# Three places of a two-layer gated cross-attention kernel: the first value block, the end of the first attention, and the LoRA tail

## The reference

```python
x = x + tanh(g_xattn[0]) * L0_xattn(layernorm(x), ctx, ctx, ...)   # rope, mask, softmax, 32 heads on 8 key heads, D = 128
x = x + tanh(g_ffn[0])   * L0_ffn(layernorm(x), ...)               # 16 experts, top 2
x = x + tanh(g_xattn[1]) * L1_xattn(layernorm(x), ctx, ...)        # RMS-normed queries and keys
x = x + tanh(g_ffn[1])   * L1_ffn(layernorm(x), ...)               # 4 LoRA experts of rank 16, top 2

# L1_ffn
logits = flat @ Wr.T                      # top 2 of 4, softmax over them: gates
mid = einsum('tf,erf->ter', flat, A)
delta = sum_e gates[:, e] * (mid_e @ B_e.T) * 4
```

## Time and profile before

| what | value |
| --- | --- |
| median of 3 runs | 1242.37 us (1242.19 to 1243.41) |
| profiled execution, own time | 1242.58 us |
| its span, first to last instruction | 1240.4 us |
| busy: PE, weight loads, DVE, ACT, POOL | 96%, 77%, 67%, 34%, 47% |

### The profile page before, as it was taken

The page is one execution under the profiler, slowest core; times in us unless marked ns, Lnnn a source line. Parts: engine busy times, 40 slices in busy tenths (PEclk is TensorE's granted clock), DMA queues, the critical chain, the costliest instruction groups (busy, mean ns, idle before and its releaser), DMA issues.

```text
span 1240.4 us, 16897 instructions
## 1 busy us (share of the span) xinstructions
PE 1194.8 (96%) x6188; PEld 949.3 (77%) x6188; DVE 828.4 (67%) x1446; ACT 423.9 (34%) x734; POOL 577.7 (47%) x399
## 2 busy tenths in 40 slices
PE   7999999899999999999899999999999999999997
PEld 6887878677777778777678887777777777777776
DVE  4656644978788887788963225586566757656795
ACT  5144151322212222222344113534444443444432
POOL 4431431757667676675344112335454545545500
PEclk9999999999999999999999999999999999999999
DMA  7844625522121221212110002122122212211101
GB/s 271 254 149 149 211 101 180 205 86 77 49 78 68 85 76 43 78 40 76 69 60 35 1 0 86 60 79 76 51 76 76 76 44 74 76 51 37 74 1 68
DMA packets 57584, 106.86 MB, mean 86 GB/s; under 512 B 3776, under 2 KB 36544, under 8 KB 52160
## 3 DMA queue, kind: packets, MB, share of 16 engines
q1 hardware_dynamic: 57008, 105.17, 24.7%
q0 software_dynamic: 384, 1.05, 0.2%
q10 hardware_dynamic: 144, 0.00, 0.0%
HBM read 78.95 MB, written 27.26 MB: 86 GB/s over the span
## 4 chain that ended last, share of the span: by engine, by line
PE 70%; DVE 13%; POOL 8%; issue 6%; ACT 3%; DMA 0%; POOLq 0%; DVEq 0%; ACTq 0%
PE ps_b L226 11%; PE ps_b L227 11%; PE ps_b L228 11%; PE ps_q L226 9%; PE ps_q L227 9%; PE ps_q L228 9%; DVE r_s L1317 3%; PE ps_b L950 2%; PE ps_s L923 2%; POOL qT L1199 2%; POOL wo_lo L1192 2%; POOL wq_lo L717 1%; PE ps_q L910 1%; POOL p_sb L769 1%; DVE o_lo L1360 1%
## 5 line engine op out<-in xcount | busy, mean ns | idle before, releaser
L226 PE MATMUL ps_q<-hT_hi,wq_hi 128*128 128x512 f32 x512 | 207.2, 405 | 4.6 <-ACT qT L1066 4.1
L227 PE MATMUL ps_q<-hT_lo,wq_hi 128*128 128x512 f32 x512 | 200.1, 391 | 0.0
L228 PE MATMUL ps_q<-hT_hi,wq_lo 128*128 128x512 f32 x512 | 199.6, 390 | 0.0
L226 PE MATMUL ps_b<-wo_hi,o_hi 128*128 128x512 f32 x440 | 172.9, 393 | 6.4 <-POOL wo_lo L1192 6.4
L227 PE MATMUL ps_b<-wo_lo,o_hi 128*128 128x512 f32 x440 | 172.1, 391 | 0.0
L228 PE MATMUL ps_b<-wo_hi,o_lo 128*128 128x512 f32 x440 | 171.9, 391 | 0.0
L1199 POOL TENSOR_TENSOR qT<-q_t 128x512 f32<-128x512 f32 x64 | 88.8, 1387 | 91.3 <-DVE q_t L1295 91.3
L226 PEld LDWEIGHTS ps_q<-hT_hi,wq_hi 128*128 128x128 f32 x512 | 96.1, 188 | 40.8 <-issue 13.5
L1360 DVE TENSOR_TENSOR o_lo<-ps_b,o_hi 128x512 fp32r<-128x512 f32 x128 | 82.1, 684 | 65.4 <-ACT o_hi L1104 64.0
L1369 DVE SCALAR_TENSOR_TENSOR x_sb<-ps_b,gates,x_sb 128x512 f32<-128x512 f32 x120 | 86.1, 724 | 52.9 <-PE ps_b L228 52.3
L717 POOL TENSOR_TENSOR wq_lo<-wq_raw,wq_hi 128x512 fp32r<-128x512 f32 x64 | 89.3, 1399 | 56.3 <-ACT wq_hi L711 56.3
(11 more groups left out here) (271 smaller groups left out, 2488.6 us busy)
## 6 DMA issues: line engine op xcount, KB each, us to landing
wq_raw<-in_wq SPq DMA_DIRECT2D x16, 1024.0 KB, 4.8
wo_raw<-in_wo SPq DMA_DIRECT2D x16, 1024.0 KB, 4.9
kT<-kT_spill SPq DMA_DIRECT2D x32, 256.0 KB, 3.4
v_hi<-v_hi_spill SPq DMA_DIRECT2D x16, 512.0 KB, 3.7
v_lo<-v_lo_spill SPq DMA_DIRECT2D x16, 512.0 KB, 4.6
v_hi_spill<-vs_hi SPq DMA_DIRECT2D x12, 512.0 KB, 5.9
v_lo_spill<-vs_lo SPq DMA_DIRECT2D x12, 512.0 KB, 6.7
kw_raw<-in_wk SPq DMA_DIRECT2D x4, 1024.0 KB, 8.9
```

The source lines that it names most:

```text
L226: nc.tensor.matmul(dst, l_hi, r_hi, start=first, stop=False)
L227: nc.tensor.matmul(dst, l_hi, r_lo, start=False, stop=False)
L228: return nc.tensor.matmul(dst, l_lo, r_hi, start=False, stop=last)
```

## The change

**Start.** TensorE runs 20 transposes of the identity into a free bank (`WARM`). Then, within a slice, high x high of all four tiles comes first, once the high parts are there, then context high x weights low, then context low x weights high.

**End of the first attention.** GpSimd subtracts the maxima of unit 14 ahead of the query addition (15, 2). VectorE does rotations 2 and 3 of unit 15 and the sums of unit 14 ahead of the last two low halves of unit 13. After the last low half of unit 15 it does output addition 0, four norms and low halves 0 and 1, then the other additions.

**Tail.** The token product takes all 128 columns of `a_raw`. Routing is done for tiles 0 to 3, then 4 to 6, then 7. ScalarE multiplies `b_raw` by `gate_l` once, so VectorE only adds. Tile 7's x is put into a bank by a product with the identity, its delta is accumulated there, and ScalarE copies the sum to x. Product 7 waits until VectorE has read the logits of tiles 4 to 6.

```diff
 def kv_pe(pe):
+    pe.wait_ge(prep["ident"], 1)
+    for n in range(WARM):                                  # WARM = 20
+        nc.tensor.transpose(ps_b[2][:, 0:P], ident[:, :], ident[:, :])
     for k in range(KC):
-        pe.wait_ge(c["w0_lo"], k + 1)
-        pe.wait_ge(prep["ctx_lo"], k + 1)
-        for i in range(4):
-            last = three(kv_banks[i][:, :], cT_hi[...], cT_lo[...], kw_hi[0][:, k, :], kw_lo[0][:, k, :], k == 0, k == KC - 1)
+        parts = (("hi", "hi"), ("hi", "lo"), ("lo", "hi"))
+        for ctx_part, w_part in parts:
+            ...
+            for i in range(4):
+                last = nc.tensor.matmul(kv_banks[i][:, :], ...)
```

```diff
 # GpSimd, att_pool, step
                 added(1)
+                if before_closing(lay, g, h):
+                    att_shift(pool, lay, us)
                 added(2)
 # VectorE, att_dve, first attention
                 rotate(last, 1, 2)
+                rotate(last, 1, 3)
+                sums(last - 1)
             out_low(last - 2, 2)
             out_low(last - 2, 3)
-            if lay == 0:
-                rotate(last, 1, 3)
-            sums(last - 1)
+            if lay:
+                sums(last - 1)
...
+            add_output(last, 1, 0)
             ln_rs(dve, ln, 0)
             ln_norm(dve, ln, 0)
             ln_norm(dve, ln, 1)
-            for t in range(PAIRS):
-                add_output(last, 1, t)
-                ln_stat(dve, ln, PAIRS + t, added)
-                for i in LN_BESIDE[t]:
-                    ln_low(dve, ln, i)
-                    if i + 2 < PAIRS:
-                        ln_norm(dve, ln, i + 2)
+            ln_stat(dve, ln, PAIRS, added)
+            ln_norm(dve, ln, 2)
+            ln_norm(dve, ln, 3)
+            ln_low(dve, ln, 0)
+            ln_low(dve, ln, 1)
+            for t in (1, 2):
+                add_output(last, 1, t)
+                ln_stat(dve, ln, PAIRS + t, added)
+            ln_low(dve, ln, 2)
+            ln_low(dve, ln, 3)
+            add_output(last, 1, 3)
+            ln_stat(dve, ln, PAIRS + 3, added)
```

```diff
 # tail
-                last = nc.tensor.matmul(bank[:, (i % PAIRS) * P:(i % PAIRS) * P + LN], xT[...], a_raw[:, k, 0:LN], ...)
+                last = nc.tensor.matmul(bank[:, (i % PAIRS) * P:(i % PAIRS + 1) * P], xT[...], a_raw[:, k, :], ...)
...
+                nc.scalar.activation(b_raw[:, :], b_raw[:, :], ACT.Copy, scale=gate_l[:, 0:1]).then_inc(lora["b_s"], 1)
...
 # lora_pe
             gated_t(0)
+            pe.wait_ge(c["route"], route_steps[PAIRS] + 1)
             lora_mid(pe, NT - 1)
-            pe.wait_ge(c["b_in"], 32)
+            pe.wait_ge(c["b_s"], 1)
             deltas(0)
+            pe.wait_ge(lora["gated"], 1)
+            nc.tensor.matmul(mid_banks[0][:, :], ident[:, :], x_sb[:, NT - 1, :], start=True, stop=False)
             gated_t(1)
             deltas(1)
 # lora_act, at its end
+            act.wait_ge(c["delta"], NT)
+            nc.scalar.activation(x_sb[:, NT - 1, :], delta_bank(NT - 1)[:, :], ACT.Copy).then_inc(c["x_last"], 1)
 # lora_dve
-            route(1)
-            dve.wait_ge(c["gate_l"], 1)
-            add_output(0)
+            route(PAIRS, NT - 1)
+            route(NT - 1, NT)
             gate(1)
-            for i in range(1, NT):
+            for i in range(NT - 1):
                 add_output(i)
```

More of the change, by code:

```diff
@@ L503, in kv_pe @@
             c = kv
+            pe.wait_ge(prep["ident"], 1)
+            for n in range(WARM):
+                nc.tensor.transpose(ps_b[2][:, 0:P], ident[:, :], ident[:, :])
             for k in range(KC):
-                pe.wait_ge(c["w0_lo"], k + 1)
-                pe.wait_ge(prep["ctx_lo"], k + 1)
-                for i in range(4):
[L509 to L512, removed]
+                parts = (("hi", "hi"), ("hi", "lo"), ("lo", "hi"))
+                for ctx_part, w_part in parts:
+                    if (ctx_part, w_part) == ("hi", "hi"):
+                        pe.wait_ge(c["w_hi"], k + 1)
+                        pe.wait_ge(prep["ctx_hi"], k + 1)
+                    elif w_part == "lo":
+                        pe.wait_ge(c["w0_lo"], k + 1)
+                    else:
+                        pe.wait_ge(prep["ctx_lo"], k + 1)
+                    for i in range(4):
+                        last = nc.tensor.matmul(kv_banks[i][:, :], (cT_hi if ctx_part == "hi" else cT_lo)[:, k, i * P:(i + 1) * P],
+                                                (kw_hi if w_part == "hi" else kw_lo)[0][:, k, :], start=k == 0 and (ctx_part, w_part) == parts[0],
+                                                stop=k == KC - 1 and (ctx_part, w_part) == parts[2])
+                        if k == KC - 1 and (ctx_part, w_part) == parts[2]:
+                            last.then_inc(c["tile"], 1)
             pe.wait_ge(prep["ctx_lo"], 2 * KC)
@@ L1942, in lora_sync @@
             for i in range(NT):
[L1943 removed]
+                sp.wait_ge(*((c["x_added"], i + 1) if i < NT - 1 else (c["x_last"], 1)))
                 sp.dma_start(ot[:, i, :], x_sb[:, i, :]).then_inc(c["out"], 16)
@@ L1991, in lora_mid @@
             for k in range(KC):
-                last = nc.tensor.matmul(bank[:, (i % PAIRS) * P:(i % PAIRS) * P + LN], xT[:, k, i * P:(i + 1) * P], a_raw[:, k, 0:LN],
+                last = nc.tensor.matmul(bank[:, (i % PAIRS) * P:(i % PAIRS + 1) * P], xT[:, k, i * P:(i + 1) * P], a_raw[:, k, :],
                                         start=k == 0, stop=k == KC - 1)
@@ L2087, in lora_act, with route @@
             gated_copy(1)
+            act.wait_ge(c["delta"], NT)
+            nc.scalar.activation(x_sb[:, NT - 1, :], delta_bank(NT - 1)[:, :], ACT.Copy).then_inc(c["x_last"], 1)
         def lora_dve(dve):
             c = lora
[L2091 to L2098 removed]
+            def route(i0, i1):
+                own, tiles, n = slice(i0, i1), range(i0, i1), i1 - i0
+                mid = mid_banks[i0 // PAIRS].rearrange("p (i m) -> p i m", m=P)[:, i0 % PAIRS:i0 % PAIRS + n, :]
+                done = route_steps[i0]
                 dve.wait_ge(c["l_clear"], 2)
[L2100 to L2101 removed]
+                dve.wait_ge(*lns[3]("rs", RS_PARTS.index((i0, i1)) + 1))
+                dve.wait_ge(c["mid"], i1)
                 nc.vector.tensor_tensor(l_lg[:, own, 0:LX], mid[:, :, LM:LN], wide(ln_rs_sb[:, own], LX), ALU.mult).then_inc(c["route"], 1)
@@ L2123, in gate @@
                 mid = mid_banks[h].rearrange("p (i m) -> p i m", m=P)
-                done = steps * h + 4 + 2 * PAIRS
+                done = gate_steps[h]
                 dve.wait_ge(c["l_ex"], h + 1)
```

45 lines of the change are left out of this document (21 added, 24 removed).

## The result

| kernel | median of its runs | lowest and highest | ratio to before, 95% interval |
| --- | --- | --- | --- |
| before | 1242.51 us (6 runs) | 1242.01, 1243.41 | |
| after | 1235.59 us (6 runs) | 1234.18, 1237.65 | 0.9945 [0.9934, 0.9956] |

What follows compares the result with a forecast made beforehand. TensorE was taken to bound the kernel, seven tenths of the last-ending chain. From the profiled 1242.58 us, start -2.3, attention's end -4.1 and tail -0.4 gave 1235.8 us, range 1234.2 to 1239.6.

Steps and rivals of the forecast that it cites:

- Start, -2.3: Program start: earlier first matmul and earlier upper clock, less a new wait, start tile 4 at 18.4 instead of 20.66 us.
- wait at tile 4: Start: the first four tiles finish close together, so tile 4 waits 0.9 us for tile 0's eviction from bank 0.
- The two slow matmuls that I allowed for: Start: the clock rises at 6.87 us, so only two real matmuls run slowly, costing 0.4 us.
- B: Rival at the start: transposes do not bring the clock forward, start gains only 0.2 us, total 1237.9 us, chance 0.28.
- Softmax, -1.95: First attention's end: GpSimd's earlier shift for unit 14 lets its transpose start at 595.35 instead of 597.30 us.
- Norms, -2.15: Norms for the MoE: VectorE's reordering brings the router product 2.15 us forward, -4.1 together with the softmax part.
- The wait ahead of the router product: MoE's start: the old wait becomes one of 1.2 us, for low half 3, ahead of the router product.
- the lower clock hardly matters: Norms stretch, clock 0.50 at 636: the new 1.2 us wait can hide it, so whether it goes hardly matters.
- Tail, -0.4: Tail: additions end at 1236.9 instead of 1237.97 us, but queued stores leave an end 0.4 us earlier.
- The upper clock in the last deltas: Tail: last deltas take about 1.0 us at the upper clock, giving -0.4; 2.08 at the lower, giving +0.4.
- only the last two stores queue for their data: Tail: two stores issued 0.45 us apart queue for their data, which reduces the gain to 0.4 us.
- a shift passes whole to the end: Between the edited stretches: TensorE has no gap or waits only on its own earlier work, so shifts reach the end whole.

Runs made afterwards that it cites:

- no_warm: The changed kernel without the twenty transposes at the start, order of the passes kept; median 1237.97 us, ratio 0.9962.
- fill: The changed kernel with transposes of the identity put into four stalls of TensorE (at 178, 245, the MoE's end, the tail); median 1232.35 us, ratio 0.9924.
- fill_before: The kernel before with transposes filling its stalls at 180, 248, the MoE's end and ahead of values 14 (601); median 1239.11 us, ratio 0.9973.
- after_again: The changed kernel run once more, nothing altered; median 1235.91 us, ratio 0.9944.
- tail_only: The kernel before with the new tail alone; median 1242.31 us, ratio 1.0 [0.999, 1.001].
- cols68: The changed kernel with 68 instead of 128 columns in the tail's token products; median 1234.40 us, ratio 0.9936.
- start_attn: The changed kernel with the old tail, so new start and attention's end only; median 1235.71 us, ratio 0.9945.
- start_only: The kernel before with the new start alone (twenty transposes, reordered passes); median 1241.56 us, ratio 0.9993 [0.9983, 1.0003].
- act01: The changed kernel with output tiles 0 and 1 also written by ScalarE through identity products, like tile 7; median 1236.55 us, ratio 0.9955.

## Why the prediction was right, point by point

**Start, -2.3: right, with a spread that I left out.** First real matmul 6.14 (6.18), wait at tile 4 0.83 (0.9), tile 4 at 18.15 (18.4). The two slow matmuls that I allowed for were none in one profile, about three in the other. B's 20.5 for tile 4 without transposes was 19.90, since eight matmuls were slow, not twelve. The rule of the Trainium skill, "TensorE: Matmul & The Clock Gate", section "Part 4: PE-mode transpose", that the upper clock doesn't engage for transposes, isn't what these runs show: without the transposes (no_warm) eight matmuls were slow that weren't in after, and in fill 26 transposes kept the granted clock at 1.00 behind 245, where after had 0.50.

**Softmax, -1.95: right.** The shift starts at 582.69, ahead of rotation 2; values 14 gained 1.9 more, and the wait is 0.75 (0.7).

**Norms, -2.15: right in the mechanism, off in size.** It measured 2.7 and 2.6 us (fill). The wait ahead of the router product is 0.98 (1.2): VectorE's chain was half a microsecond shorter than my sum. But I didn't ask what the low clock of before cost there. By fill_before, where it didn't fall, 1.46 of the 2.6 are the clock that fell behind the wait of 1.73, and 1.2 the reordering itself. So over half of the term was that the edit took a stall away. My sentence that the lower clock hardly matters spoke of the kernel after, where the new wait would hide it; no profile of a kernel with this edit has the low clock there, so it stays untested.

**Tail, -0.4: about right, by wrong steps.** Filled, the new tail is 0.2 us faster than the old (1232.35 and 1232.54), which their runs hardly tell apart. The upper clock in the last deltas was a chance: up in after, down in after_again. And I let only the last two stores queue for their data, while all eight leave within 5 us and take 2.3 us to land instead of 2.0 in fill, tail_only and cols68. The new tail took 26.5 to 26.6 us from its first token products in tail_only, cols68, no_warm and fill, the old one 26.9 to 27.7 in the six kernels that have it. In five of these the clock fell before the last delta had ended, and the sixth has the long end told below, so no two profiles compare the tails at equal clocks. Between before and fill it is 0.3 us.

The 28.3 us of after are not the tail's order. Between fill's profile and after's, the stores' end differs by 1.7 us. Here are windows of 1 us in after behind its last delta, the share of its DMA queues from 1224.3 to 1233.3 us, and a window of fill behind its last delta:

```profile
1228.00:1229.00 1.00, 0.00 (x0) 0.00 (x0) 0.09 (x1) 0.00 (x0) 0.00 (x0) 1.00 0.56 211
1231.00:1232.00 1.00, 0.00 (x0) 0.00 (x0) 0.00 (x0) 0.00 (x0) 0.00 (x0) 0.81 0.28 105
1232.00:1233.00 1.00, 0.00 (x0) 0.00 (x0) 0.00 (x0) 0.00 (x0) 0.00 (x0) 0.50 0.03 12
...
q8 instruction: 1, 0.02, 0.9%
```

```profile
1228.00:1229.00 1.00, 0.00 (x0) 0.00 (x0) 0.00 (x0) 0.00 (x0) 0.00 (x0) 1.00 1.02 387
```

In after the traffic halves once amid the stores and trickles at their end, and a packet of 16 KB of the instruction queue lies among them. Three of the fourteen profiles have such a packet while stores are under way: after, after_again and start_attn. In these three 3.9 to 5.2 us pass from the last write of x to the end of the span. In the other profiles with the new tail it is 3.3 to 3.5 us, in the other ones with the old tail 2.5. So the long end goes with that packet, in the old tail as in the new, and the new one's own price at the stores is 0.8 to 1.0 us, which its earlier last write makes up for. No run moves the packet, so that it is the cause is not shown.

**What the sum didn't have.** The MoE's end (-1.64 in after) is no term of it. In the profile the start brought -2.5, the softmax part -1.8, the norms -2.7, the MoE's end with small shifts behind it -1.5, and the tail +1.4: in all -7.1. I had said that a shift passes whole to the end, since TensorE runs without a gap between the stretches. That step failed: start_only kept 1.0 of its 2.4 us up to 590, and each of the eight unfilled profiles with those edits won 1.6 to 1.7 at the MoE's end, which I hadn't counted. The total came out right by luck: 1.5 at the MoE's end and 0.7 more than computed in the three first terms, against 1.8 less in the tail.

## What to carry to other kernels

When an edit shifts a program, compare the granted clock behind every stall of TensorE (here the clock fell behind some of 1.7 to 3.7 us) before a gain is put to the edit; in after and start_only the same stall ended 0.14 us apart, and they differ by 1.3 us of clock behind it. Where TensorE has to wait anyway, work into a free bank can keep its clock: 54 transposes in three stalls and ten in the tail took the median down by 3.2 us, where the whole hand-made change took 6.9. And price an edit with the stalls filled in both kernels, since then the runs of one kernel lie within about 1 us.

## What the runs showed of the hardware

The same wait of 3.7 us was followed by seven slow matmuls in after, eight in before and thirteen in start_only, though it began within 2.5 us in all three. A wait of 1.93 us cost 1.6 us of clock in before, and one of 1.94 nothing in after; one of 2.3 us at 178 cost 1.6 in cols68, act01 and no_warm and nothing in before and after. Twenty transposes took 4.53 us at the start of after and 26 took 3.00 at 241.65 in fill: 0.23 and 0.12 us each, the two levels of the clock, while the window at 8 us printed 1.00 over slow matmuls in before. So at the start the spacing shows the clock and the printed column doesn't.
